# A four-layer network on one core: the small experts of its third layer get four weight sets, and part of the shared expert's work is done between the two expert loops

## What is computed

```python
logits = x @ Wg.T ; sig = sigmoid(logits)
topk_idx = top_k(sig + e_bias, 6)                  # 6 experts for each token
topk_w = 2.5 * sig[topk_idx] / sum(sig[topk_idx])
for e in experts:                                  # at most 192 tokens each
    g, u = split(x[tokens of e] @ W_gate_up[e])    # 192 -> 2 * 464
    y = (silu(g) * u) @ W_down[e]                  # 464 -> 192
    routed[tokens of e] += topk_w * y
shared = silu(x @ Wsg) * (x @ Wsu) @ Wsd           # 192 -> 928 -> 192
out = routed + shared
```

## Time and profile before

| | before |
|---|---|
| median of 3 runs | 841.12 us (840.67 to 842.9) |
| profiled execution, its own time | 844.89 us |
| its span, first to last instruction | 843.0 us |
| first loop, third layer | 463.4 to 567.1 us of the span |
| second loop, with its first products | 569.8 to 607.0 us |
| tail | 607.1 to 635.2 us |
| granted TensorE clock, mean | 0.940 |

### The profile page before, as it was taken

One profiled execution on the slowest core, in us unless ns is written; L12 is line 12 of the kernel. 1 busy time (PEld: TensorE's weight loads), 2 busy tenths in 40 slices (PEclk: granted clock), 3 DMA queues, 4 the chain that ended last, 5 costly groups with the idle time before them and its releaser, 6 DMA issues. The chain is left out here.

```text
span 843.0 us, 15814 instructions
## 1 busy us (share of the span) xinstructions
PE 749.0 (89%) x5369; PEld 558.3 (66%) x5369; DVE 378.4 (45%) x1111; ACT 306.2 (36%) x723; POOL 273.4 (32%) x316
## 2 busy tenths in 40 slices
PE   8996999798999988999977899997898967989885
PEld 5774888465585657999744788873455656666663
DVE  1354222234263257788595122221153695645543
ACT  2530222223464047666331122222234453524440
POOL 0004455100002116676023544443301161045770
PEclk9997999998989999999999999999999889879995
DMA  9815889400000052220041879626554030811224
GB/s 355 337 32 166 275 276 289 144 1 1 1 3 1 0 215 70 70 75 14 1 148 31 296 240 391 194 55 207 195 126 160 29 99 3 315 41 53 69 73 98
DMA packets 39254, 108.50 MB, mean 129 GB/s; under 512 B 5616, under 2 KB 12736, under 8 KB 38672
## 3 DMA queue, kind: packets, MB, share of 16 engines
q1 hardware_dynamic: 31584, 88.35, 30.7%
q0 software_dynamic: 7600, 19.25, 8.6%
HBM read 95.88 MB, written 11.70 MB: 128 GB/s over the span
## 5 line engine op out<-in xcount | busy, mean ns | idle before, releaser
L1431 POOL TENSOR_TENSOR ssm_w_low<-ssm_wbc,ssm_w_high 128x512 fp32r<-128x512 f32 x24 | 31.1, 1300 | 38.5 <-ACT ssm_w_high L1386 38.5
L157 ACT ACT_TABLE_LOAD x19 | 24.4, 1283 | 49.1 <-PEq L162 48.9
L2056 POOL TENSOR_TENSOR L_s_up<-L_s_hid,L_s_up 116x288 f32<-116x288 f32 (+1 forms) x10 | 8.3, 828 | 103.6 <-ACT L_s_up L2050 103.6
L1836 DVE TENSOR_TENSOR L_act_many<-L_hid,bank 116x384 f32<-116x384 f32 x28 | 15.5, 554 | 57.0 <-ACT L_hid L1716 44.8
L1346 PE MATMUL bank<-ssm_x_high,ssm_w_high 128*128 128x288 f32 x96 | 33.8, 352 | 3.8 <-DVE bank L1474 2.3
L1441 POOL TENSOR_TENSOR ssm_grown<-ssm_less,xn 128x576 f32<-128x576 f32 x23 | 32.9, 1430 | 8.0 <-ACT ssm_less L1414 5.3
L1691 POOL DMA_INDIRECT y_rows_L<-L_many_y,L_many_rows_out x21 | 20.7, 988 | 44.4 <-ACT L_many_y L1734 37.1
L1716 ACT ACTIVATE L_hid<-bank 116x384 f32<-116x384 f32 x28 | 13.7, 490 | 56.8 <-PE bank L1767 38.4
L1480 DVE TENSOR_TENSOR_SCAN ssm_state<-ssm_decay,bank 128x576 f32<-128x576 f32 x24 | 32.5, 1354 | 0.8
L2025 PE MATMUL bank<-xn,par_L1f 128*116 128x288 f32 (+1 forms) x128 | 31.0, 455 | 0.1
L1666 POOL DMA_INDIRECT L_many_xr<-x_rows_L,L_many_rows_in x27 | 26.8, 994 | 11.9 <-issue 10.6
(11 more groups left out here) (550 smaller groups left out, 1938.4 us busy)
## 6 DMA issues: line engine op xcount, KB each, us to landing
L_w<-in_L2w SPq DMA_DIRECT2D x14, 696.0 KB, 7.1
L_more<-in_L2w SPq DMA_DIRECT2D x10, 696.0 KB
L_w<-in_L0w SPq DMA_DIRECT2D x12, 576.0 KB
ssm_wbc<-in_wBC SPq DMA_DIRECT2D x24, 256.0 KB
L_w<-in_L3w SPq DMA_DIRECT2D x5, 1152.0 KB
L_w<-in_L2w SPq DMA_DIRECT2D x14, 384.0 KB
L_more<-in_L0w SPq DMA_DIRECT2D x9, 576.0 KB
second<-in_L3w SPq DMA_DIRECT2D x16, 291.0 KB
```

The source lines that it names most:

```text
L157: self.nc.scalar.activation(self.unread[:, at:at + 1], self.p["ones"][:, 0:1], func)
L1431: pool.tensor_tensor(w_low[t % NW][:, :], wbc[t % NW][:, :], w_high[t % NW][:, :], ALU.subtract).then_inc(low, 1)
```

## The change

`Few` gets four weight sets instead of two (`TURN = 4`): its own two, and as third and fourth those of `Many`. A set's weights are now loaded four steps ahead. The third and fourth set are loaded for the first time between the two loops, the first weights once all up products of the first loop are made and the second weights once all its down products are. The body of the loop is written out for four steps in a row instead of two; the smallest count is 7 experts, and the plan has four more places. Four of the 16 shared products of the tail (`BETWEEN = 4`) are made on PE between the loops, behind the first `turn` of `Few`, and taken by ACT ahead of its first gates. Both counts are read by each engine at the start of the block. The vector engine writes the two counts with two instructions instead of one.

```diff
-LEAST = 3
-MANY_PLACES, FEW_PLACES = 2 * (MANY_STEPS + 2), 2 * (FEW_STEPS + 2)
+MANY_PLACES, FEW_PLACES = 2 * (MANY_STEPS + 2), 2 * (FEW_STEPS + 4)
+BETWEEN = 4
...
     def steps_in_use(self, eng, n, body):
 
+        turns = GROUP * SETS // self.TURN
+
         def group(g):
-            with eng.Fori(0, GROUP) as i:
-                r = i + g * GROUP
-                q = r * SETS
-                with eng.If(q * 2 < n):
-                    body(r, q, 0)
-                    with eng.If((q + 1) * 2 < n):
-                        body(r, q + 1, 1)
+            with eng.Fori(0, turns) as i, ExitStack() as nest:
+                r = i + g * turns
+                for s in range(self.TURN):
+                    q = r * self.TURN + s
+                    nest.enter_context(eng.If(q * 2 < n))
+                    body(r * (self.TURN // SETS) + s // SETS, q, s % SETS, r, s)
...
-    def sp(self, sp, after=None):
-        U, n = self.UNITS, self.in_use(sp)
-
-        def step(r, q, h):
-            with self.comes(sp, n, q + 2):
+    def sp(self, sp, n, after=None):
+        U, ahead = self.UNITS, self.TURN
+
+        def step(half, q, h, r, s):
+            with self.comes(sp, n, q + ahead):
                 e = []
                 for j in range(2):
                     sp.wait_ge(self.up, q * self.GATES + self.LAST_UP[j])
-                    e.append(self.load_first(sp, (q + 2) * 2 + (self.place + j), 2 * h + j))
+                    e.append(self.load_first(sp, (q + ahead) * 2 + (self.place + j), 2 * s + j))
                 for j in range(2):
                     sp.wait_ge(self.down, q * U + self.LAST_DOWN[j])
-                    self.load_second(sp, e[j], 2 * h + j)
+                    self.load_second(sp, e[j], 2 * s + j)
...
         self.turn(pe, 0, 0, 1)
+        shared.first(pe, 1, 0, 0, BETWEEN)
         pe.wait_ge(self.xt_in, 1)
+        self.turn(pe, 1, 0, 1)
         for j in range(2):
             pe.wait_ge(self.loaded[j], 16)
-        self.turn(pe, 1, 0, 1)
-        self.upwards(pe, 0)
+        pe.wait_ge(shared.out, 2 * shared.C + 2)
+        self.upwards(pe, 0, 0)
+        pe.wait_ge(shared.out, 2 * shared.C + BETWEEN)
         self.steps_in_use(pe, n, step)
...
-        for k, loop in enumerate((many, few)):
-            loop.buffers(ctx, X.w1[2 * k:2 * k + 2] + [more1[:, 2 * k + j, :] for j in range(2)],
-                         X.w2[2 * k:2 * k + 2] + [more2[:, 2 * k + j, :] for j in range(2)])
+        slots = [(X.w1[2 * k:2 * k + 2] + [more1[:, 2 * k + j, :] for j in range(2)],
+                  X.w2[2 * k:2 * k + 2] + [more2[:, 2 * k + j, :] for j in range(2)]) for k in range(2)]
+        many.buffers(ctx, *slots[0])
+        few.buffers(ctx, slots[1][0] + slots[0][0], slots[1][1] + slots[0][1])
...
         def _(sp):
+            n, n_few = many.in_use(sp), few.in_use(sp)
             many.load(sp, 1)
-            steps = [(many, many.sp(sp, few)), (few, few.sp(sp))]
...
+            many.sp(sp, n, few)
+            sp.wait_ge(many.up, (n + 1) // 2 * 4)
+            sp.sem_inc(many.noted, 1)
+            e = [few.load_first(sp, few.place + 4 + j, 4 + j) for j in range(4)]
+            sp.wait_ge(many.down, (n + 1) // 2 * 3)
+            sp.sem_inc(many.noted, 1)
+            for j in range(4):
+                few.load_second(sp, e[j], 4 + j)
+            few.sp(sp, n_few)
...
         def _(pe):
+            n, n_few = many.in_use(pe), few.in_use(pe)
             pe.sem_inc(many.y_in, many.AT_FIRST)
             pe.sem_inc(few.y_in, few.AT_FIRST)
             many.turn(pe, 0, 0, 1)
             many.turn(pe, 0, 1, 1)
-            n = many.pe(pe)
+            many.pe(pe, n)
             pe.wait_ge(many.xt_in, (n + 1) // 2 * 3 + 2)
             pe.sem_inc(many.noted, 1)
-            few.pe(pe)
+            few.pe(pe, n_few)
             tail.pe(pe)
...
         def _(act):
+            n, n_few = many.in_use(act), few.in_use(act)
             many.take_gates(act, many.experts_of(act, many.place), 0, 1)
-            many.act(act)
-            few.act(act)
+            many.act(act, n)
+            X.shared.take(act, 1, 0, 0, BETWEEN)
+            few.act(act, n_few)
             tail.act(act)
```

More of the change, by code:

```diff
@@ L1864, in upwards @@
             for j, rows in enumerate(self.ROWS):
-                mm = pe.matmul(banks[a][rows, 0:I], self.xt[h][half, 1, rows], self.w1[2 * h + j][half, 2 * I:3 * I], start=False, stop=True)
+                mm = pe.matmul(banks[a][rows, 0:I], self.xt[h][half, 1, rows], self.w1[2 * s + j][half, 2 * I:3 * I], start=False, stop=True)
             mm.then_inc(made, 1)
@@ L1882, in downwards, with pe, step @@
         for j in range(2):
-            pe.wait_ge(self.loaded_second[2 * h + j], r * 16 + 16)
+            pe.wait_ge(self.loaded_second[2 * s + j], r * 16 + 16)
         for f in range(X.C):
             for j, rows in enumerate(self.ROWS):
-                mm = pe.matmul(bank[rows, 0:DIM], X.act_few[:, f, rows], self.w2[2 * h + j][0:X.N, DIM * f:DIM * f + DIM],
+                mm = pe.matmul(bank[rows, 0:DIM], X.act_few[:, f, rows], self.w2[2 * s + j][0:X.N, DIM * f:DIM * f + DIM],
                                start=(f == 0), stop=(f == X.C - 1))
         mm.then_inc(self.down, 1)
-    def pe(self, pe):
-        n = self.in_use(pe)
-        def step(r, q, h):
+    def pe(self, pe, n):
+        shared = self.X.shared
+        def step(half, q, h, r, s):
             self.turn_hidden(pe, q, h)
@@ L2036, in second, with take @@
             mm.then_inc(self.down, 1)
-    def take(self, act, s, bank):
+    def take(self, act, s, bank, start=0, end=None):
         if s:
             act.wait_ge(self.down, 2)
-        for u in range(2 * self.C):
+        for u in range(start, end or 2 * self.C):
             v = self.C * s + u // 2
@@ L2251, in act @@
             return
-        self.X.shared.take(act, 1, 0)
+        self.X.shared.take(act, 1, 0, self.begun)
         for i in range(TILES):
@@ L2275, in pe @@
             return
-        self.X.shared.first(pe, 1, 0, 0, 2 * self.X.shared.C)
+        self.X.shared.first(pe, 1, 0, self.begun, 2 * self.X.shared.C)
         self.X.shared.second(pe, 1, 4)
@@ L2621, in _ @@
             dve.scalar_tensor_tensor(start[:, :], at_many[:, 1:2], is_few, at_many[:, 0:1], ALU.mult, ALU.add).then_inc(based, 1)
-            dve.tensor_scalar(X.plan[0:1, P:P + 2], T.bank[2][0:1, 4:6], float(LEAST), None, ALU.max).then_inc(plan_known, 1)
+            for i, loop in enumerate((X.many, X.few)):
+                ins = dve.tensor_scalar(X.plan[0:1, P + i:P + i + 1], T.bank[2][0:1, 4 + i:5 + i], float(loop.LEAST), None, ALU.max)
+            ins.then_inc(plan_known, 1)
             dve.tensor_tensor(place_many[:, 0:1], got[:, 0:1], is_many, ALU.mult)
@@ L2724, in _ @@
         def _(sp):
+            n, n_few = many.in_use(sp), few.in_use(sp)
             many.load(sp, 1)
-            steps = [(many, many.sp(sp, few)), (few, few.sp(sp))]
-            for loop, n in steps:
-                for j in range(2 * SETS):
+            many.sp(sp, n, few)
[7 more added lines that the diff above has]
+            few.sp(sp, n_few)
+            for loop, used in ((many, n), (few, n_few)):
+                for j in range(2 * loop.TURN):
                     for loaded in (loop.loaded[j], loop.loaded_second[j]):
-                        sp.wait_ge(loaded, loop.uses(n, j // 2) * 16)
+                        sp.wait_ge(loaded, loop.uses(used, j // 2, loop.TURN) * 16)
             sp.sem_inc(many.noted, 1)
```

86 lines of the change are left out of this document (41 added, 45 removed).

## The result

The changed kernel took 848.0 us (median of 4 runs, 842.8 to 852.12), the kernel before 840.89 beside it: a ratio of 1.0088, 95% interval 1.0047 to 1.0129. Where 836.2 was forecast, and at most 840.4, it is some 7 us slower. Repeated twice, the ratio was 1.0111 and 1.0089.

The account below looks back on a forecast made before the run. Second-loop weight waits, the seam's stand and slow clock, and TensorE's tail chain bound the block. Seam 3.5 later, sets 5.8 and tail 3.7 earlier, less 0.2, 0.1, 0.8: 4.9 faster, 841.1 to 836.2 us; range 832.8 to 840.4.

Parts of the forecast that it names:

- The four sets: Second loop: no waits for weights, four steps cost 20.5 us instead of 26.32, so 5.8 us earlier.
- The tail: Third layer's tail: 12 shared units instead of 16, 3.7 us earlier; TensorE's and the fetch chain end almost together.
- The last wait for a gather: Second loop's last turn: its wait of 1.34 us for a gather stays.
- The start: Start of the block: counts read ahead of the first turn make the first loop start 0.9 us later.
- The wait of 6.3 us in the first step: First loop: DVE stood 6.30 us for ACT; the slower rival had this wait return at the seam.
- The engine stands 2.1 us instead of 2.7: Seam between the loops: TensorE stands 2.1 us instead of 2.7, with the same 1.6 charged for slow clock.
- I take 0.8: Leaving the second loop: cost 0 to 2.1 us for an exit jumping over three steps, taken as 0.8.
- the 2.71: Seam: TensorE's 2.71 us "issue" gap between the loops; one count read falling away there was to save 0.57.
- Places and branches else: 0, since TensorE's sequencer is ahead of its matmuls inside a step: All other code places and branches: the change was to cost nothing there, 0 us.
- the 4.9 that was forecast: Whole kernel: 6.0 us earlier in all, less 0.2, 0.1 and 0.8, gives 4.9 us faster.
- a rival on jumps: Second loop's exit and jump back: jumps into longer code cost, gain only 2.8, so 838.3 us; chance 0.20.
- The rival on the slower side: Seam: full DMA engines bring back the 6.3 us wait plus 1.5 clock, 2.9 slower, 844.0 us; chance 0.09.

Follow-up runs that it names:

- before_again: The unchanged kernel run once more for a second trace and its spread: 842.09 us, ratio 0.9974 to the kernel before.
- two_sets: Changed kernel with two weight sets, a two-step second-loop body and no loads at the seam; reads and shared products stay: 842.76 us, ratio 1.0025.
- before_one_copy: Kernel before with each expert loop's code once and 33 never-executed matmuls keeping the last loop at its old place: 840.15 us, ratio 1.0015.
- one_copy_placed: Changed kernel with each expert loop's code once, plus 54 never-executed matmuls putting the last loop at the place before: 833.25 us, ratio 0.9895.
- one_copy_loops: Changed kernel with each expert loop's code standing once, its number of turns taken from the count: 836.09 us, ratio 0.9941 to the kernel before.

## Why the prediction was wrong

*What held.* The four sets: 20.2 us for four steps where 20.5 was forecast, no wait for weights. The tail: 12 units in 11.07 us, and the second sum begins when its fetch lands. The last wait for a gather: 1.67 for 1.34. The start: the first product of the first loop (463.69) comes 1.0 later behind the shared products than before; 0.9 was forecast. The wait of 6.3 us in the first step isn't in this trace, nor in that of before_again.

*What was mis-sized.* "The engine stands 2.1 us instead of 2.7" at the seam: it stood 3.35 to 4.67 in six traces. "I take 0.8" for the exit, from a range of 0 to 2.1: it stood 2.39 to 2.72, and the branch that is slow there jumps over the second copy of the loop's code, not over three steps. I had read the 2.71 as partly the read of a count; two_sets, without that read, still stood 1.77, and with the code once the stand is gone, with the read (before_one_copy) as without. That the block came out as forecast in spite of this is partly chance: without the 6.3 us wait, the first loop's last matmuls ended 4.1 us earlier than in the trace that I had counted from (563.03 for 567.10). Over six traces the block is 165.4 long, 4.2 less than the 169.6 of before. The wait of 6.3 us seems to have cost the kernel before nothing: in before_again, without it, the first loop ends at 562.99, but the second then waits longer for weights (4.63 instead of 3.72, again with half clock behind it), and the block is as long.

*The step that failed* is "Places and branches else: 0, since TensorE's sequencer is ahead of its matmuls inside a step". Inside a step that held: the steps are 5.05 apart and TensorE doesn't stand for a branch in them. But the change moves all the code behind it, and a far branch 200 us later got 3 us longer. The 3.0 of stand and what comes with it in the clock are the largest part of the loss: taking this one place back brought 9 to 11 us, from 848 to 850 down to 839.4. That is 1.5 us under the kernel before by the ratio, which the measurement can't tell from nothing. The rest of the 4.9 that was forecast fits the longer stands at the seam and the exit: with these gone as well (one_copy_placed) the kernel is 1.05% faster than the one before. I had a rival on jumps, but only for jumps in the loops that the diff touches, and asked nowhere what else stands behind the added code. The rival on the slower side (full DMA engines when the engines jump to the second loop) was near the mark: they cost TensorE 2 us of branch. The wait of 6.3 us between ACT and DVE that it named wasn't seen there, and this rival wasn't what decided.

*Open.* The dead code alone moves the median by 5 to 11 us where the traces show 3 of stand. The rest comes together with a lower mean clock: over the 116 timings of the kernel before that stand beside these runs, 0.01 less of mean clock goes with some 6 us more. Why dead code lowers it isn't shown, and which stretches lose it in the usual execution the traces don't settle: six profiled executions of the changed kernel took 839.7 to 847.6, mostly less than the usual 848 to 850. Why the fourth layer's clock before its last loop was lower too (0.85 for 0.87 over the whole stretch) wasn't separated from the stand.

## What to carry to other kernels

When a change adds instructions to an engine's program, list the far jumps of that engine behind it, however far away and unrelated, and compare their stands ("issue" in the row behind a loop) before crediting or blaming the change itself. Dead code behind a branch can move them back at the price of one near branch (under 0.4 us here), and so separates what a change does from where it puts the rest. Code that stands once, with the number of turns taken from the count, needed no far jump at these two loops. The jump took longest here where the DMA engines were full, so big loads are better issued behind it.

## What the runs showed of the hardware

- A far branch on TensorE took 3.3 to 4.4 us where loads didn't fill the DMA engines (share 0.18 to 0.42 during the branches of before and after) and 5.0 to 6.2 where they did (0.96 in after); a near one at most 0.36. At the last loop's place of before, where a 16 KB packet had started before the branch (818.35, the branch at 819.36), it took 1.0 to 1.9.
- Each of the long branches ended 2.3 to 2.9 us after the start of a 16 KB instruction packet on TensorE's queue. With the DMA engines full at the seam that packet started 2.6 to 3.9 us into the branch, otherwise 1.0 to 1.2.
- Even where the branch is short (0.34), TensorE stood 2.60 us soon behind the target, until 2.4 us after a 16 KB packet started (one_copy_loops).
- Only TensorE's sequencer had branches over 0.5 us; those of the other four engines stayed under 0.4 us in all 18 traces.
- 84 instructions that are never executed cost 5 us of 842 (ratio 1.0089).
